# Decoder layer on one core: key norms read from the Gram matrix's diagonal on VectorE, two key products moved inside the first projection, the second state products given a bank of their own

## The chip, the cores and the metric

The kernel runs on one core of a Trainium2 chip. The metric is the device time of one execution in microseconds (us). Five engines work side by side, each through its own list of instructions in order: TensorE (PE in the rows, its weight loads PEld), VectorE (DVE), ScalarE (ACT), GpSimd (POOL), and SyncE (SP), which only issues transfers. They meet through semaphores.

## What is computed

One decoder layer for 4 sequences of 512 tokens with 512 features: a gated delta rule attention with 16 heads, a small cross attention over 64 sets, and a feed-forward part with ternary weights. The change lies in the attention:

```
q = silu(conv(h @ Wq)); k = silu(conv(h @ Wk)); v = silu(conv(h @ Wv))     # DK = 96, DV = 192
q = l2norm(q) * DK ** -0.5;  k = l2norm(k)         # x * rsqrt(sum(x * x) + 1e-6)
beta = 2 * sigmoid(h @ Wb);  g = -exp(A_log) * softplus(h @ Wa + dt_bias)
for every token:
    S = S * exp(g);  delta = (v - k @ S) * beta;  S = S + outer(k, delta);  o = q @ S
o = rmsnorm(o) * norm_weight * silu(h @ Wg);  out = x + o @ Wo
```

The kernel never normalizes the key itself. It divides what is made of the key by sum(k * k) + EPS, so every token needs that sum.

## The kernel before

The attention (`stage_delta_rule`) takes a head's 512 tokens in four chunks of 128, for all four sequences at once. One call of `step(st)` on each engine is one chunk of one head: 64 full steps n, with chunk c = n % 4, written out one after another, with no loop on the chip. A step overlaps the stages of several chunks. It projects and convolves chunk n + 2 (three jobs of 128 features, `projection`, `tap0`, `conv`, `tanh`, `silu`), prepares chunk m = n + 1 ("turn": the key's Gram matrix, the decay differences, the transposes to tokens, the triangular inverse), runs the recurrence on chunk n ("recur"), and projects the output of chunk n - 1.

Each engine's order is written by hand: the calls in TensorE's `step`, and the lists of (condition, function) at the end of ScalarE's and VectorE's `step`. `past` and `hold` are waits on a semaphore for a value.

The places that matter here, in the order of a step:

- `keys(st)`, TensorE. ScalarE's `key_squares` squares the key (96 features x 512 tokens) into the tile `junk`. TensorE multiplies it with a column of ones, four products with one column each (L705), and gets sum(k * k) per token in bank 2. Then four products key by key (L710) fill bank 6 with the Gram matrix of each sequence.
- `exponent_sums(st)`, TensorE (L692): the decay differences into bank 5, which ScalarE's `decay` turns into `E` (L985).
- `keyscale`, VectorE (L1171, L1177, L1183): from the sums in bank 2 it makes `nsse` = -(sum + EPS), its reciprocal, and `Dn` = reciprocal times beta. `masked` (L1259) then makes the lower triangular matrix `LT` = Gram x Dn x E.
- GpSimd: the norm factor of the previous chunk (`ms`, `rn`), then `Gm` for the next decay differences (L592), then `UB` from `Dn` (L599), `Em` (L604), the scaled keys `K2` (L636).
- `y_16` (L737) and `x_16` (L744, L745), TensorE: the first two levels of the inverse. `y_16` waits until the inverse's 16 x 16 blocks have come back through HBM as `X` and `XT` (L550), `x_16` waits for VectorE's `Y16` (L1161). The blocks are inverted on 32 partitions by VectorE's `recursion` late in the step before.
- `add_x(i)`, VectorE (L1309): adds one sequence's projected output to x. The delta products (`V`, `XT`, L800) reuse those banks and wait for it.
- At the end of a step: the state products K2 x Dl (L800), two pairs of sequences, pair 0 into bank 4 and pair 1 into bank 7. Bank 7 still holds the second pair of output gates until VectorE's `gate_pair(1)` (L1238) has read them, so pair 1 waits for that. In chunk 3 there are no state products: the state starts anew with the next head, and VectorE only clears S (L1280). VectorE's order at the end of the step is silu of job 2, `gate_pair(1)`, two `out_pair` (L1247 or L1249), `state` (L1275).

The line numbers are those of the kernel before.

## Time and profile before

| | |
|---|---|
| median of three runs | 2714.29 us (2713.38 to 2724.97) |
| the profiled execution's own time | 2716.69 us |
| its span in the trace | 2714.9 us |
| TensorE busy | 2516.7 us, 93% |
| VectorE busy | 2068.5 us, 76% |
| ScalarE busy | 1362.4 us, 50% |
| GpSimd busy | 900.5 us, 33% |
| attention with all of its stages running (135 to 2150 us): TensorE busy | 1952.2 of 2015.0 us |
| granted TensorE clock there | 0.99 |

The table gives totals. The rows below give places: a row of a timeline is a run of equal instructions with its start in the span and its length, and in square brackets how long its engine stood idle just before it and which instruction ended that. A TensorE row's end is modelled, since matmuls are pipelined, so TensorE's time is best read from the start of one row to the start of the next.

### The profile page before, as it was taken

Reading aid. Unit: us, or ns where it says so; the run is one execution under the profiler, and the core shown is the slowest. Engines: PE = TensorE matmul, PEld = TensorE weight load, DVE = VectorE, ACT = ScalarE, POOL = GpSimd, SP = SyncE. Lnnn points to the kernel's source line nnn. Section 1 sums busy time; section 2 is a strip of 40 time slices with the busy share of each in tenths; the row PEclk is TensorE's granted clock in tenths of the full one; section 3 lists DMA queues with packets and bytes.
Section 4 is the critical chain, followed back from the end, with each engine's and each line's share of the span. In section 5 each row is a group of like instructions: output and inputs, shape, how many; then the busy total and the mean of one; then the engine's idle time right before and its main releaser. Section 6 shows DMA issues by size and latency. Waiting matters only on the chain. (4 is left out here: it accounts for less than half of the span.)

```text
span 2714.9 us, 55951 instructions
## 1 busy us (share of the span) xinstructions
PE 2516.7 (93%) x20408; PEld 1698.7 (63%) x20408; DVE 2068.5 (76%) x5037; ACT 1362.4 (50%) x3171; POOL 900.5 (33%) x1210
## 2 busy tenths in 40 slices
PE   4599999999999999999999999999999999877998
PEld 3367676766666666676666676666666666653443
DVE  6577778887878787878787878788887878456776
ACT  2245455555555555555555555554545444323555
POOL 0223333333333233333333333333333323113544
PEclk8789899999999999999999999999999999687999
DMA  2211111111211111222222222221111010030000
GB/s 86 61 36 47 46 49 47 49 47 49 47 47 45 44 39 38 55 52 56 54 57 55 57 54 57 55 56 34 33 30 31 20 32 18 13 121 1 20 20 24
DMA packets 289341, 120.78 MB, mean 44 GB/s; under 512 B 211462, under 2 KB 267046, under 8 KB 288556
## 3 DMA queue, kind: packets, MB, share of 16 engines
q1 hardware_dynamic: 289068, 117.21, 16.9%
q8 instruction: 163, 2.67, 0.4%
q14 instruction: 110, 0.90, 0.1%
HBM read 85.42 MB, written 31.74 MB: 43 GB/s over the span
## 5 line engine op out<-in xcount | busy, mean ns | idle before, releaser
L1125 DVE SCALAR_TENSOR_TENSOR d_y<-bank,d_cw,d_y 128x508 f32<-128x508 f32 (+2 forms) x576 | 422.6, 734 | 146.3 <-ACT d_y L923 136.5
L622 POOL TENSOR_SCALAR d_ms<-d_sso 128x4 f32<-128x4 f32 x64 | 14.5, 227 | 911.5 <-ACT d_junk L1056 911.5
L642 POOL TENSOR_TENSOR d_sq<-d_tok 128x384 f32<-128x384 f32 x64 | 52.8, 826 | 509.9 <-ACT d_tok L976 509.9
L1041 ACT ACTIVATE d_thg<-bank 128x384 f32<-128x384 f32 x128 | 61.6, 481 | 311.7 <-PE bank L788 311.6
L923 ACT ACTIVATE d_y<-bank,d_cw 128x512 f32<-128x512 f32 x192 | 131.5, 685 | 141.2 <-PE bank L669 140.0
L1309 DVE SCALAR_TENSOR_TENSOR x<-bank,x 128x512 f32<-128x512 f32 x256 | 171.8, 671 | 21.4 <-PE bank L831 21.4
L976 ACT ACTIVATE d_tok<-bank 128x384 f32<-128x384 f32 x256 | 125.5, 490 | 54.0 <-PE bank L684 50.0
L1151 DVE SCALAR_TENSOR_TENSOR d_yv<-d_th,d_y 128x512 f32<-128x512 f32 x128 | 88.9, 694 | 81.0 <-ACT d_th L930 80.4
L930 ACT ACTIVATE d_th<-d_y 128x512 f32<-128x512 f32 x192 | 119.6, 623 | 55.5 <-DVE d_tail L1136 55.4
L636 POOL TENSOR_SCALAR d_K<-d_tok,d_Em 128x96 f32<-128x96 f32 x256 | 144.0, 578 | 0.1
L1133 DVE SCALAR_TENSOR_TENSOR d_y<-d_tail,d_cw,d_y 128x4 f32<-128x4 f32 (+2 forms) x432 | 123.7, 286 | 15.3
L1056 ACT ACTIVATE d_junk<-d_O 128x192 f32<-128x192 f32 x256 | 89.6, 351 | 88.8 <-DVE d_O L1249 66.5
L831 PE MATMUL bank<-d_wo1h,d_onT 128*128 128x512 f16 x384 | 129.5, 392 | 3.5 <-ACT d_onT L1068 3.5
L788 PE MATMUL bank<-d_wgh,hhi 128*128 128x192 f16 x1024 | 127.1, 247 | 0.0
L788 PE MATMUL bank<-d_wgl,hhi 128*128 128x192 f16 x1024 | 126.4, 246 | 0.0
L788 PE MATMUL bank<-d_wgh,hlo 128*128 128x192 f16 x1024 | 126.4, 246 | 0.0
L831 PE MATMUL bank<-d_wo0h,d_onT 128*128 128x512 f16 x384 | 125.7, 382 | 0.0
L614 POOL TENSOR_TENSOR d_V<-d_tok,d_kinv 128x640 f32<-128x640 f32 (+1 forms) x128 | 124.2, 991 | 0.0
L669 PE MATMUL bank<-hhi,d_wa0h 128*128 128x512 f16 x384 | 102.8, 392 | 19.3 <-DVE d_wa0l L1102 16.2
L800 PE MATMUL bank<-d_Dl,d_K 128*96 128x192 f32 x384 | 82.7, 338 | 36.2 <-DVE d_gate L1238 34.4
L1665 POOL TENSOR_TENSOR f_zv<-f_zv,f_zg 128x512 f32<-128x512 f32 x64 | 86.8, 1357 | 86.3 <-DVE f_zv L1831 57.0
L800 PE MATMUL bank<-d_V,d_XT 128*128 128x192 f32 x512 | 108.7, 335 | 6.3 <-DVE x L1309 6.3
(281 smaller groups left out, 7010.1 us busy)
## 6 DMA issues: line engine op xcount, KB each, us to landing
lt_blocks<-d_LT SPq DMA_DIRECT2D x64, 256.0 KB, 2.4
d_fw<-turned_gate_w SPq DMA_DIRECT2D x32, 256.0 KB, 3.2
d_XT<-x_blocks SPq DMA_DIRECT2D x128, 64.0 KB, 2.4
d_X<-x_blocks SPq DMA_DIRECT2D x128, 64.0 KB, 2.5
d_fw<-turned_val_w SPq DMA_DIRECT2D x32, 256.0 KB, 3.2
d_fw<-turned_out_w SPq DMA_DIRECT2D x32, 256.0 KB, 2.9
d_st<-in_L_attn_Wg_dram SPq DMA_DIRECT2D x16, 384.0 KB, 4.7
ternary<-d_ft SPq DMA_DIRECT2D x48, 128.0 KB, 2.1
```

The source lines that it names most:

```text
L614: last = nc.gpsimd.tensor_tensor(V[q][:, :, lo:hi], tok[q][:, :, at:at + hi - lo], over(kinv[:, :], 2, hi - lo), ALU.mult)
L636: nc.gpsimd.tensor_scalar(K2[:, i, :], tok[st.p][:, i, K_AT:K_AT + DK], Em[st.p][:, i, P - 1:P], None, ALU.mult).then_inc(s["K2_ready"], 1)
L669: last = nc.tensor.matmul(acc[:, :], wa[st.wp][w][:, k, t * P:(t + 1) * P], x[:, k, :].rearrange("p (b t) -> p b t", b=B)[:, :, st.cp * P: ...
L788: last = nc.tensor.matmul(bank[(4, 7)[pair]][:, i * DV:(i + 1) * DV], x[:, k, tile * P:(tile + 1) * P], wg[w][:, k, :], start=(e == 0), st ...
L800: last = nc.tensor.matmul(bank[at][0:rows, i * DV:(i + 1) * DV], lhsT(e), rhs(e), start=True, stop=True)
L831: last = nc.tensor.matmul(bank[(4, 7, 6, 5)[i]][:, :], o, w, start=(e == 0), stop=(e == len(terms) - 1))
L923: nc.scalar.activation(y[(st.p + j) % 2][:, :, :].rearrange("p b t -> p (b t)"), bank[(st.p + j) % 2][:, :], ACT.Copy, scale=cw[:, ds(st.k ...
L930: nc.scalar.activation(th[:, :, :], y[(st.p + j) % 2][:, :, :], ACT.Tanh).then_inc(s["tanh_done"], 1)
L976: nc.scalar.activation(tok[st.pm][:, i, :], bank[2][:, 0:QKV], ACT.Copy).then_inc(s["tok_read"], 1)
L1125: nc.vector.scalar_tensor_tensor(out=yy[:, :, tap:], in0=pp[:, :, 0:P - tap], scalar=cw[:, ds(st.kp, 1), t, 3 - tap], in1=yy[:, :, tap:], ...
L1133: nc.vector.scalar_tensor_tensor(out=yy[:, :, 0:back], in0=old[:, :, 3 - back:], scalar=cw[:, ds(st.kp, 1), t, 3 - back], in1=yy[:, :, 0:b ...
L1309: nc.vector.scalar_tensor_tensor(out=xs, in0=bank[(4, 7, 6, 5)[i]][:, :], scalar=1.0 / (SO * SW), in1=xs, op0=ALU.mult, op1=ALU.add).then_ ...
```

## The change

It has three parts. The sums of the squared keys are no longer computed by ScalarE and TensorE: VectorE multiplies the Gram matrix in bank 6 with an identity, into `diag` (the tile `junk` again), and sums each row. The Gram products and the decay differences move up to between the first and second third of the first projection, with VectorE's `keyscale` and `masked` ahead of the convolution, and ScalarE's `decay` ahead of `tap0`. The second pair of state products goes to bank 2, and VectorE's `gate_pair(1)` moves behind `state`. A one-time step for the ternary weights (`magnitudes`) leaves `keyscale` and runs once, later.

```diff
@@ VectorE, keyscale and its place
-                def keyscale(i):
-                    if i == 0:
-                        v.wait_ge(s["key_done"], 2 * m + 1)
-                        nc.vector.tensor_scalar(nsse[:, :], bank[2][:, 3 * P:3 * P + B], EPS, -1.0, ALU.add, ALU.mult).then_inc(s["Dn_ready"], 1)
...
+                def keyscale():
+                    v.wait_ge(s["key_done"], m + 1)
+                    past(v, "ssq_done", B * n)
+                    nc.vector.tensor_tensor(diag, bank[6][:, :].rearrange("p (b t) -> p b t", b=B), over(ident, 1, B), ALU.mult).then_inc(s["Dn_ready"], 1)
+                    v.wait_ge(s["Dn_ready"], 5 * m + 1)
+                    nc.vector.tensor_reduce(nrec[:, :], diag, AXX, ALU.add).then_inc(s["Dn_ready"], 1)
+                    v.wait_ge(s["Dn_ready"], 5 * m + 2)
+                    past(v, "kappa_done", 4 * m - 2)
+                    nc.vector.tensor_scalar(nsse[:, :], nrec[:, :], EPS, -1.0, ALU.add, ALU.mult).then_inc(s["Dn_ready"], 1)
...
-                for go, what in ((P_, lambda: conv(st, 0, 1)), (T_, lambda: keyscale(0)), (T_, lambda: keyscale(1)), (T_, lambda: keyscale(2)),
-                                 (T_, masked), (R_, y16), (P_, lambda: conv(st, 0, 2)), (R_, products), (P_, lambda: conv(st, 0, 3)),
+                for go, what in ((T_, keyscale), (T_, masked), (R_, y16), (P_, lambda: conv(st, 0, 1)), (P_, lambda: conv(st, 0, 2)), (R_, products), (P_, lambda: conv(st, 0, 3)),
...
-                                 (R_, lambda: gate_pair(1)), (R_, lambda: out_pair(0)), (R_, lambda: out_pair(1)), (R_, state)):
+                                 (R_, lambda: out_pair(0)), (R_, lambda: out_pair(1)), (R_, state), (R_, lambda: gate_pair(1))):
@@ TensorE, keys
-                past(pe, "tok_read", B * m)
-                hold(pe, s["ksq_done"], m + 1)
...
-                for i in range(B):
-                    last = nc.tensor.matmul(bank[2][:, 3 * P + i:3 * P + i + 1], ksq[:, i, :], cst[0:DK, C_U + P - 1:C_U + P], start=True, stop=True)
-                last.then_inc(s["key_done"], 1)
+                past(pe, "silu_done", 3 * m + 1)
                 past(pe, "LT_ready", B * m)
                 past(pe, "O_ready", 2 * st.n - 1)
@@ TensorE, queries
                 past(pe, "S_ready", B * n + B)
+                past(pe, "gate_ready", 2 * n)
@@ TensorE, step
-                proj(0)
+                proj(0, 0, 3)
                 if st.turn:
+                    keys(st)
                     exponent_sums(st)
-                    keys(st)
+                proj(0, 1, 3)
+                proj(0, 2, 3)
...
-                if c < CH - 1:
-                    past(pe, "gate_ready", 2 * n + 2)
-                pair_of(st, "su_done", 1, 7, lambda i: K2[:, i, :], lambda i: Dl[:, i, :], rows=DK, product=c < CH - 1)
+                if st.turn:
+                    past(pe, "tok_read", B * n + 2 * B)
+                pair_of(st, "su_done", 1, 2, lambda i: K2[:, i, :], lambda i: Dl[:, i, :], rows=DK, product=c < CH - 1)
@@ ScalarE
-            def key_squares(st):
...
-                nc.scalar.activation(ksq[:, :, :], yv[st.pm][0:DK, 1, :, :], ACT.Square).then_inc(s["ksq_done"], 1)
-                    past(a, "key_done", 2 * n + 3 if st.turn else 2 * n + 1)
+                    past(a, "Dn_ready", 5 * n + 7 if st.turn else 0)
-                for go, what in ((T_, lambda: key_squares(st)), (P_, lambda: tap0(st, 0)), (T_, decay), (True, lambda: heads(0)), (T_, lambda: jobs(0)), (R_, copy_x32), (T_, lambda: tokens(st, 0)),
+                for go, what in ((T_, decay), (P_, lambda: tap0(st, 0)), (True, lambda: heads(0)), (T_, lambda: jobs(0)), (R_, copy_x32), (T_, lambda: tokens(st, 0)),
```

On TensorE, at the border of the second and third full step, the program before has this order. The rows from the state products on (their left operand is `K`, their right one `Dl`, in the rows' names `d_Dl,d_K`) are the end of one step and the start of the next.

```order
L800 MATMUL bank<-d_Dl,d_K 96x192 x4
L669 MATMUL bank<-hhi,d_wa1h 128x512 x4
L669 MATMUL bank<-hhi,d_wa1l 128x512 x4
L669 MATMUL bank<-hlo,d_wa1h 128x512 x4
L692 MATMUL bank<-d_Gm,cst 128x512
L705 MATMUL bank<-cst,d_junk 128x1 x4
L710 MATMUL bank<-d_yv 128x128 x4
L737 MATMUL bank<-d_X,d_LT 64x32 x8
L719 MATMUL bank<-d_qT,d_yv 128x128 x4
```

The changed program has this at the same border.

```order
L798 MATMUL bank<-d_Dl,d_K 96x192 x4
L669 MATMUL bank<-hhi,d_wa1h 128x512 x4
L707 MATMUL bank<-d_yv 128x128 x4
L697 MATMUL bank<-d_Gm,cst 128x512
L669 MATMUL bank<-hhi,d_wa1l 128x512 x4
L669 MATMUL bank<-hlo,d_wa1h 128x512 x4
L735 MATMUL bank<-d_X,d_LT 64x32 x8
L717 MATMUL bank<-d_qT,d_yv 128x128 x4
```

The one-column products are gone, and the Gram products and the decay differences stand two thirds of a projection earlier.

On VectorE, from the last silu of a step (`d_yv<-d_th`) through the first products of the next, the program before has this order.

```order
L1151 SCALAR_TENSOR_TENSOR d_yv<-d_th,d_y 128x512
L1238 SCALAR_TENSOR_TENSOR d_gate<-d_thg,bank 128x384
L1249 TENSOR_TENSOR d_O<-bank,d_Q 128x384 x2
L1275 SCALAR_TENSOR_TENSOR d_S<-d_S,dec,bank 96x192 x4
L1125 SCALAR_TENSOR_TENSOR d_y<-bank,d_cw,d_y 128x4x127
L1171 TENSOR_SCALAR d_nsse<-bank 128x4
L1177 RECIPROCAL d_nrec<-d_nsse 128x4
L1183 TENSOR_TENSOR d_Dn<-d_nrec,sc 128x4
L1259 SCALAR_TENSOR_TENSOR d_LT<-bank,d_Dn,d_E 128x128 x4
L1161 SCALAR_TENSOR_TENSOR d_Y<-bank,cst 128x4x16 x2
L1125 SCALAR_TENSOR_TENSOR d_y<-bank,d_cw,d_y 128x4x126
L1267 TENSOR_TENSOR d_PT<-bank,d_Em 128x512
```

The changed program has this there.

```order
L1144 SCALAR_TENSOR_TENSOR d_yv<-d_th,d_y 128x512
L1245 TENSOR_TENSOR d_O<-bank,d_Q 128x384 x2
L1270 SCALAR_TENSOR_TENSOR d_S<-d_S,dec,bank 96x192 x4
L1234 SCALAR_TENSOR_TENSOR d_gate<-d_thg,bank 128x384
L1163 TENSOR_TENSOR d_junk<-bank,cst 128x512
L1165 TENSOR_REDUCE d_nrec<-d_junk 128x4
L1168 TENSOR_SCALAR d_nsse<-d_nrec 128x4
L1170 RECIPROCAL d_nrec<-d_nsse 128x4
L1172 TENSOR_TENSOR d_Dn<-d_nrec,sc 128x4
L1254 SCALAR_TENSOR_TENSOR d_LT<-bank,d_Dn,d_E 128x128 x4
L1154 SCALAR_TENSOR_TENSOR d_Y<-bank,cst 128x4x16 x2
L1118 SCALAR_TENSOR_TENSOR d_y<-bank,d_cw,d_y 128x4x127
```

The gate stands behind the state update, two instructions are new, and the first tap of the convolution (L1125 before, L1118 now) comes after all of the key's work.

## Rows read from the trace of the kernel before

**Rows 1.** The page: its head, and the engines' busy times.

```profile
span 2714.9 us, 55951 instructions
PE 2516.7 (93%) x20408; PEld 1698.7 (63%) x20408; DVE 2068.5 (76%) x5037; ACT 1362.4 (50%) x3171; POOL 900.5 (33%) x1210
```

**Rows 2.** Timeline of TensorE, end of a chunk 0, start of its chunk 1.

```profile
1291.30 0.89 PE L800 MATMUL bank<-d_Dl,d_K 128*96 128x192 f32 x4 [0.94 <-DVE d_gate L1238]
1292.03 1.03 PE L669 MATMUL bank<-hhi,d_wa0h 128*128 128x512 f16 x4
...
1294.62 1.02 PE L692 MATMUL bank<-d_Gm,cst 128*128 128x512 f32 x2
1295.48 0.95 PE L705 MATMUL bank<-cst,d_junk 96*128 96x1 f32 x8
1296.29 1.14 PE L710 MATMUL bank<-d_yv 96*128 96x128 f32 x8
1297.36 0.66 PE L737 MATMUL bank<-d_X,d_LT 64*64 64x32 f32 x16
...
1299.20 0.31 PE L744 MATMUL bank<-d_Y,d_XT 64*64 64x32 f32 x4
```

**Rows 3.** The page's group of the state products: busy, mean ns | idle before.

```profile
L800 PE MATMUL bank<-d_Dl,d_K 128*96 128x192 f32 x384 | 82.7, 338 | 36.2 <-DVE d_gate L1238 34.4
```

**Rows 4.** Timeline of VectorE over the same border and into chunk 1.

```profile
1291.16 1.02 DVE L1247 COPY d_O<-bank 128x384 f32<-128x384 f32 x2
...
1292.10 1.37 DVE L1275 SCALAR_TENSOR_TENSOR d_S<-d_S,dec,bank 96x192 f32<-96x192 f32 x4
...
1295.60 0.75 DVE L1125 SCALAR_TENSOR_TENSOR d_y<-bank,d_cw,d_y 128x508 f32<-128x508 f32 x1 [2.13 <-ACT d_y L923]
...
1296.88 0.16 DVE L1183 TENSOR_TENSOR d_Dn<-d_nrec,sc 128x4 f32<-128x4 f32 x1
...
1298.68 0.46 DVE L1161 SCALAR_TENSOR_TENSOR d_Y<-bank,cst 128x64 f32<-128x64 f32 x2
...
1299.71 0.68 DVE L1267 TENSOR_TENSOR d_PT<-bank,d_Em 128x512 f32<-128x512 f32 x1
...
1312.35 0.55 DVE L1286 TENSOR_REDUCE d_ss<-d_sq 128x4 f32<-128x384 f32 x1 [0.95 <-POOL d_sq L642]
...
1315.13 0.69 DVE L1151 SCALAR_TENSOR_TENSOR d_qT<-d_th,d_y 128x512 f32<-128x512 f32 x1 [2.04 <-ACT d_th L930]
```

**Rows 5.** Timeline of TensorE in the chunk 0 before it.

```profile
1256.36 1.03 PE L669 MATMUL bank<-hhi,d_wa0h 128*128 128x512 f16 x4
...
1260.88 1.02 PE L705 MATMUL bank<-cst,d_junk 96*128 96x1 f32 x8 [0.78 <-ACT d_junk L954]
...
1284.84 0.89 PE L800 MATMUL bank<-d_V,d_XT 128*128 128x192 f32 x4 [0.42 <-DVE x L1309]
```

**Rows 6.** Timeline of VectorE in that chunk 0.

```profile
1257.37 0.55 DVE L1238 SCALAR_TENSOR_TENSOR d_gate<-d_thg,bank 128x384 f32<-128x384 f32 x1
1257.84 1.02 DVE L1249 TENSOR_TENSOR d_O<-bank,d_Q 128x384 f32<-128x384 f32 x2
...
1262.41 0.32 DVE L1183 TENSOR_TENSOR d_Dn<-d_nrec,sc 128x4 f32<-128x4 f32 x1
1263.12 1.13 DVE L1259 SCALAR_TENSOR_TENSOR d_LT<-bank,d_Dn,d_E 128x128 f32<-128x128 f32 x4 [0.39 <-PE bank L710]
...
1265.19 0.68 DVE L1267 TENSOR_TENSOR d_PT<-bank,d_Em 128x512 f32<-128x512 f32 x1
...
1283.91 0.67 DVE L1309 SCALAR_TENSOR_TENSOR x<-bank,x 128x512 f32<-128x512 f32 x1
```

**Rows 7.** Timeline of GpSimd in that chunk 0.

```profile
1260.08 0.23 POOL L622 TENSOR_SCALAR d_ms<-d_sso 128x4 f32<-128x4 f32 x1 [14.98 <-ACT d_junk L1056]
...
1261.67 1.04 POOL L592 TENSOR_TENSOR d_Gm<-cst,sc 128x512 f32<-128x512 f32 x1
...
1264.30 1.27 POOL L604 TENSOR_TENSOR d_Em<-d_E,d_UB 128x512 f32<-128x512 f32 x1
```

**Rows 8.** SyncE's last load of blocks in chunk 1.

```profile
1292.38 0.62 SPq L550 DMA_DIRECT2D d_X<-x_blocks  x1
```

**Rows 9.** The same in chunk 0.

```profile
1259.00 0.62 SPq L550 DMA_DIRECT2D d_X<-x_blocks  x1
```

**Rows 10.** The page's DMA issues: KB each, median us to landing.

```profile
d_X<-x_blocks SPq DMA_DIRECT2D x128, 64.0 KB, 2.5
```

**Rows 11.** Windows: busy times, PEclk, DMA share, GB/s of two chunk 0 steps.

```profile
275.00:313.50 38.50, 36.36 (x274) 24.74 (x275) 30.05 (x71) 17.40 (x44) 13.52 (x16) 0.82 0.12 31
...
420.00:453.50 33.50, 30.63 (x276) 21.15 (x276) 29.92 (x71) 17.68 (x46) 13.76 (x16) 1.00 0.14 32
```

More of the change, by code:

```diff
@@ L595, in key_decay @@
             def key_decay(m, q):
-                hold(pool, s["Dn_ready"], 3 * m + 3)
+                hold(pool, s["Dn_ready"], 5 * m + 5)
                 past(pool, "Em_ready", m)
@@ L679, in to_tokens @@
                     past(pe, "silu_done", 3 * m + 3)
-                    past(pe, "Dn_ready", 3 * m + 1)
                 past(pe, "tok_read", B * m + i)
+                if i == 0 and st.n == TERN - 1:
+                    past(pe, "fsum_ready", 1)
+                    for e, at in enumerate((C_U, C_GT)):
+                        last = nc.tensor.matmul(bank[2][:, 3 * P + 8:3 * P + 8 + N_W], cst[:, at:at + P], fall[:, :], start=(e == 0), stop=(e == 1))
+                    last.then_inc(s["fgam_done"], 1)
+                    past(pe, "fsum_ready", 2)
                 for t in range(3):
@@ L697, in keys @@
                 m, key = st.n + 1, yv[st.pm][0:DK, 1, :, :]
-                past(pe, "tok_read", B * m)
-                hold(pe, s["ksq_done"], m + 1)
-                if st.n == TERN - 1:
-                    past(pe, "fsum_ready", 1)
-                    for e, at in enumerate((C_U, C_GT)):
-                        nc.tensor.matmul(bank[2][:, 3 * P + 8:3 * P + 8 + N_W], cst[:, at:at + P], fall[:, :], start=(e == 0), stop=(e == 1))
-                for i in range(B):
-                    last = nc.tensor.matmul(bank[2][:, 3 * P + i:3 * P + i + 1], ksq[:, i, :], cst[0:DK, C_U + P - 1:C_U + P], start=True, stop=True)
-                last.then_inc(s["key_done"], 1)
+                past(pe, "silu_done", 3 * m + 1)
                 past(pe, "LT_ready", B * m)
@@ L824, in output @@
                     past(pe, "qs_read", B * n + 2 * i + 2)
-                if i < 2 and st.c == 0:
+                if i < 2 and not st.recur:
                     past(pe, "gate_ready", 2 * n - 1 + i)
@@ L1148, in silu @@
                     past(v, "ks_done", 2 * st.n + 2 if st.recur else 0)
-                    past(v, "ksq_done", st.n + 1)
+                    past(v, "key_done", st.n + 1)
                     dst = yv[st.p][:, t - 1, :, :]
@@ L1185, in square, with magnitudes @@
+                def magnitudes():
+                    v.wait_ge(s["fgam_done"], 1)
+                    nc.vector.tensor_scalar(gam[:, :], bank[2][:, 3 * P + 8:3 * P + 8 + N_W], 1.0 / (FF * D), 1e-5,
+                                            ALU.mult, ALU.max).then_inc(s["fsum_ready"], 1)
+                    v.wait_ge(s["fsum_ready"], 2)
+                    nc.vector.reciprocal(rgam[:, :], gam[:, :]).then_inc(s["gam_ready"], 1)
                 def square(tile, w, row, col):
@@ L1275, in state @@
                             nc.vector.scalar_tensor_tensor(out=S[:, i, :], in0=S[:, i, :], scalar=dec[0:DK, ds(n, 1), i],
-                                                           in1=bank[(4, 7)[i // 2]][0:DK, (i % 2) * DV:(i % 2 + 1) * DV],
+                                                           in1=bank[(4, 2)[i // 2]][0:DK, (i % 2) * DV:(i % 2 + 1) * DV],
                                                            op0=ALU.mult, op1=ALU.add).then_inc(s["S_ready"], 1)
```

32 lines of the change are left out of this document (9 added, 23 removed).

## The prediction, made before the changed kernel was run

> **What bounds the kernel now.** I read the page first. TensorE is busy for 93% of the span and VectorE for 76% [rows 1], and in the attention TensorE's rows follow each other almost without a gap. So I look for two things: TensorE work that goes away, and the few places where TensorE stands idle. Then I ask of the others only whether they are still in time when TensorE comes earlier.
>
> The timeline of TensorE at the start of a chunk 1 shows both. The second pair of state products begins after 0.94 us idle, which VectorE's gate ended. From the one-column products (1295.48) to the Gram products (1296.29) 0.81 us pass, and to the next row, 1297.36, 1.07 us more [rows 2]. The page's group of the state products adds the idle up: 36.2 us over the run, 34.4 of it ended by the gate [rows 3]. It occurs in chunks 0, 1 and 2.
>
> VectorE in the same stretch has room: 2.13 us idle before its first tap, and again 0.95 and 2.04 us before it takes up the second silu [rows 4]. In chunk 0 it is otherwise. There the delta products of TensorE stand idle for 0.42 us until VectorE's `add_x` [rows 5]. VectorE has little room, since it also makes two low halves of weights in that chunk. So TensorE paces chunks 1 to 3, and VectorE the middle of chunk 0.
>
> **The change part by part.** *The one-column products.* They go, in 63 full steps that prepare a next chunk: 63 x 0.81 = 51.0 us.
>
> *The second state pair.* It no longer waits for the gate. Its new wait, for the tokens that were read from bank 2, was met long before. That frees 36.2 us, if nothing else is late next.
>
> *What VectorE must now do, in chunk 1.* The two outputs start where the gate stood, 0.46 us earlier, at 1290.7. By the row starts the state follows 0.94 us later, at 1291.6, and ends 1.37 us after that, at 1293.0. The gate (0.55, as in [rows 6]) ends at 1293.5. Only then comes the new work, which the trace doesn't show. The nearest row to the product with the identity is `PT`, a product of one bank with one tile over 512 columns: 0.68 us. The nearest to the sum is the reduce over 384 columns: 0.55 us, by columns 0.73 for 512 [rows 4]. Low end for the two together: 1.2, if both hide part of their start behind each other. High end: 3.5, if each stands behind one GpSimd instruction of 1.04 [rows 7]. I take 1.4, the rows' own times, since `PT` ran in 0.68 beside GpSimd's `Em` [rows 6, 7]. That is 1294.9. The small ones take some 0.2 us each, so `Dn` is there at 1295.5, `LT` 1.1 later [rows 6], `Y16` 0.46 after that: 1297.1.
>
> *What TensorE asks of it.* The projection starts at 1292.03 - 0.94 = 1291.1. One third of 2.59 is 0.86, then the Gram products 1.07, the decay differences 0.86 (1294.62 to 1295.48), and the other two thirds 1.73: `y_16` begins at 1295.6 instead of 1297.36. `x_16`, which needs `Y16`, comes 1.84 later, at 1297.4 [rows 2]. VectorE is in time by 0.3 us. So its 1.4 us are hidden, in idle time that was 2.13 us; without that cover they cost 1.4 us a step, 88 us in all. Behind `Y16` stand all three taps, but the 0.95 and 2.04 us of idle further on take them up [rows 4].
>
> *A collision.* In chunk 0, `Dn` took 0.32 us and ended at 1262.73, just as GpSimd's `Gm` did (1261.67 + 1.04 = 1262.71); in chunk 1, beside no such row, it took 0.16 [rows 4, 6, 7]. It has two inputs in SBUF. Now `Dn` comes earlier and so meets `Gm` in each chunk: some 0.25 us of the 0.3 in chunk 1. By the Trainium skill, page "SBUF — State Buffer", section "Who interferes with whom", a VectorE instruction with two SBUF inputs is blocked by a GpSimd instruction that reads SBUF, one with at most one such input outside the two-port modes is not. The trace agrees in `Dn` and `PT`; by that rule the identity product and the sum, each with one SBUF input, would not be held.
>
> *The blocks' return.* The last load in chunk 1 is issued at 1292.38 and lands 2.5 later, at 1294.9, before `y_16` at 1295.6 [rows 8, 10]. In chunk 0 it is 1259.00 + 2.5 = 1261.5 [rows 9, 10], against a `y_16` at 1261.6 (below). That is near, but not late.
>
> *Chunk 0.* TensorE is through the first third at 1256.36 + 0.86 = 1257.2 [rows 5]. The Gram products now need bank 6, which the first output frees at 1257.37 + 0.55 = 1257.9 [rows 6]: 0.7 us of new wait, where before 0.78 us went by before the one-column products [rows 5]. These two cancel. With 1.07 + 0.86 + 1.73 `y_16` stands at 1261.6. VectorE's `Dn` lies behind `Gm`, which itself starts some 0.4 earlier (the squares of the output on ScalarE follow the output): 1262.3 against 1262.73. But the first tap, which stood ahead of it, now stands behind, with 0.7. So `PT` begins as before, within 0.2 us, and so do the second half's instructions, `add_x` among them. TensorE, some 0.8 us early, waits for it at the delta products and gives back 0.6 us: 15 x 0.6 = -9 us. After that wait its next gain, the second state pair, counts fully.
>
> *Once.* The ternary scales move behind VectorE's `w_pair`, and TensorE's first transposes of that step wait for them: -1.6 us. ScalarE loses `key_squares` and gains nothing. It is not on the path outside chunk 0.
>
> *The sum.* 51.0 + 36.2 - 9 - 1.6 = 76.6 us. From the profiled execution's 2716.7 us (span 2714.9) that gives 2640.1. The median stands 2.4 us below the profiled execution, so I predict 2638 us.
>
> **The rivals.** *The removed products were nearly free* (0.10). They had one column each, and their 0.81 us could be time in which the array only waits for weights that another group would then wait for. For it speaks that eight passes of one column can hardly fill 0.81 us. Against it: the Gram group behind has its own weights, and the same spacing of about 0.1 to 0.13 us a pass [rows 2]. A quarter left, 63 x 0.2 = 13 us, gives 2676. The Trainium skill, page "TensorE: Matmul & The Clock Gate", section "Wait — 56ns, not 53.3ns?", puts the smallest spacing of matmuls at about 25 ns, so eight would cost 0.2 us and 63 steps 12.6 us; the row says 0.81, and I go by the row.
>
> *VectorE's new pair lands behind GpSimd* (0.14). `rn` and `Gm` run just then. One such row, 1.04 us [rows 7], less what is in hand, makes `x_16` wait about 0.8 in chunks 1 and 2 and 0.5 in chunk 3, whose border gains less, and delays VectorE by 0.8 in chunk 0: 2.9 us a head, 46 us, 2684. `PT` beside `Em` speaks against it.
>
> *More* (0.12). If VectorE's idles in chunk 0 (0.39 before `LT` [rows 6]) absorb more than I think, the 9 us stay. And the state pair's idle is counted from a modelled end: the pair's row is 0.89 long, yet the next begins 0.73 after it [rows 2], so each of 48 waits may have been 0.16 longer, 7.7 us in all. Both together: 2621.
>
> *Slower: the clock falls* (0.05). Two chunk 0 steps of the same kind took 38.50 and 33.50 us, at a mean granted clock of 0.82 and 1.00: in the first TensorE spent part of the stretch at 1.2 GHz instead of 2.4 [rows 11]. A fall costs 5.0 us. What set it off I can't read from the rows. The changed chunk 0 bunches its waits: 0.7 before the Gram products, more than 1 before the delta products. If that brings a fall in each of 15 chunks 0, the 75 us are gone (2713); from the 16th on it is slower, and with every second chunk 1 as well (23 falls) it would be 2753. Against it: TensorE's waits elsewhere shrink.
>
> *No change* (0.03): the state pair's wait comes back in full at `y_16`, for blocks that land later, and the rest in chunk 0.
>
> **How the numbers follow.** The forecast, 2624 to 2650, has 0.56. Its own spread is that of either half of the case of more, and of a wait of 0.2 us at `x_16` in 60 steps. Below it lies that case in full with 0.12, above it the two partial gains with 0.24. From 2618 to 2684 I leave out the clock, the no-change case and the tails, less than 2 in 10. 0.5% is 13.6 us, about what a measurement of this kernel tells from no change, so faster means below 2700.7: 0.93. The clock case divides, and gives slower 0.04, same 0.03.
>
> **What would show it.** In the changed trace: no idle before the second state pair; 0.86 us from the first projection row to the Gram products in chunks 1 to 3; the identity product at 0.68 and the sum near 0.7; `Dn` ending where `Gm` ends; `x_16` without more than 0.2 us of wait; and in chunk 0 a wait of a good 1 us before the delta products, where it was 0.42. A head (four steps) should take 4.9 us less. I am wrong if `x_16` waits for `Y16` by half a microsecond or more, if `y_16` waits for the blocks, or if the granted clock leaves 1.00 in the middle of the attention.

## The result, and the profile after

The changed kernel takes 2633.36 us (median of 4 runs, 2629.04 to 2639.26), the kernel before in the same comparison 2713.93 us (2713.38 to 2724.97). The ratio is 0.9695, with an interval of 0.9663 to 0.9727. The forecast was 2638 us in a range of 2618 to 2684. The profiled execution took 2630.96 us.

The head of the page, beside [rows 1]:

```profile
span 2629.2 us, 54834 instructions
PE 2435.9 (93%) x19896; PEld 1631.3 (62%) x19896; DVE 2179.0 (83%) x5165; ACT 1325.9 (50%) x3107; POOL 903.6 (34%) x1210
```

The span is 85.7 us shorter. TensorE's busy time is down by 80.8 us at the same share, and VectorE's is up by 110.5: it now makes the key's sums that ScalarE and TensorE made.

The timeline of TensorE at the border into a chunk 1 answers to [rows 2]:

```profile
1241.70 1.46 PE L798 MATMUL bank<-d_Dl,d_K 128*96 128x192 f32 x8
1243.00 1.03 PE L669 MATMUL bank<-hhi,d_wa0h 128*128 128x512 f16 x4
1243.87 1.06 PE L707 MATMUL bank<-d_yv 96*128 96x128 f32 x8
1244.76 1.02 PE L697 MATMUL bank<-d_Gm,cst 128*128 128x512 f32 x2
...
1247.44 0.65 PE L735 MATMUL bank<-d_X,d_LT 64*64 64x32 f32 x16
1248.03 1.16 PE L717 MATMUL bank<-d_qT,d_yv 96*128 96x128 f32 x8
1249.77 0.31 PE L742 MATMUL bank<-d_Y,d_XT 64*64 64x32 f32 x4 [0.58 <-DVE d_Y L1154]
```

Both state pairs are now one row of eight, with no idle inside. The projection starts 1.30 us after the first of them. The Gram products follow 0.87 us later. But the last line has a bracket that [rows 2] did not have: `x_16` stands idle for `Y16`.

VectorE in the same stretch, beside [rows 4]:

```profile
1243.79 1.38 DVE L1270 SCALAR_TENSOR_TENSOR d_S<-d_S,dec,bank 96x192 f32<-96x192 f32 x4
1245.08 0.54 DVE L1234 SCALAR_TENSOR_TENSOR d_gate<-d_thg,bank 128x384 f32<-128x384 f32 x1
1245.55 0.68 DVE L1163 TENSOR_TENSOR d_junk<-bank,cst 128x512 f32<-128x512 f32 x1
1246.26 0.69 DVE L1165 TENSOR_REDUCE d_nrec<-d_junk 128x4 f32<-128x512 f32 x1
1246.98 0.78 DVE L1168 TENSOR_SCALAR d_nsse<-d_nrec 128x4 f32<-128x4 f32 x1
1247.79 0.18 DVE L1170 RECIPROCAL d_nrec<-d_nsse 128x4 f32<-128x4 f32 x1
1248.01 0.16 DVE L1172 TENSOR_TENSOR d_Dn<-d_nrec,sc 128x4 f32<-128x4 f32 x1
1248.20 1.13 DVE L1254 SCALAR_TENSOR_TENSOR d_LT<-bank,d_Dn,d_E 128x128 f32<-128x128 f32 x4
1249.24 0.47 DVE L1154 SCALAR_TENSOR_TENSOR d_Y<-bank,cst 128x64 f32<-128x64 f32 x2
```

and GpSimd, beside [rows 7]:

```profile
1245.68 1.04 POOL L627 TENSOR_TENSOR d_rn<-d_ms,d_mhalf 128x4 f32<-128x4 f32 x1
1246.69 1.04 POOL L592 TENSOR_TENSOR d_Gm<-cst,sc 128x512 f32<-128x512 f32 x1
```

Read the two together. `nsse` has four columns and takes 0.78 us; it ends at 1247.76, and `Gm` ends at 1247.73. In chunk 0 it is `Dn` (1214.39, 0.76 us, to 1215.15) that ends with `Gm` (1215.14). The product with the identity (0.68) and the sum (0.69), which lie beside `rn` and `Gm` as well, are not held.

TensorE's waits over the attention (135 to 2250 us; total us, times, longest):

```profile
PE bank L742 <- DVE d_Y L1154: 20.5, 42, 0.9
PE bank L707 <- DVE d_O L1245: 10.6, 16, 0.7
PE bank L751 <- ACT d_XT L989: 6.6, 14, 0.6
PE bank L798 <- DVE x L1304: 6.3, 15, 0.4
PE bank L735 <- DMA d_X<-x_blocks: 5.2, 12, 1.2
```

The gate's wait of [rows 3] is off the list but for one of 2.7 us at the start. `x_16` (L742) waits in its place, for 20.5 us. The last line is new as well: `y_16` now waits at times for the blocks to come back, where the kernel before had no such wait.

GpSimd's L622 runs once a step and serves as a clock for all that follows: I take the distance from one to the next as the length of a step, and the median of each of the four kinds over the middle of the attention. The same head, before and after:

```profile
1293.41 0.23 POOL L622 TENSOR_SCALAR d_ms<-d_sso 128x4 f32<-128x4 f32 x1 [12.93 <-ACT d_junk L1056]
...
1433.35 0.23 POOL L622 TENSOR_SCALAR d_ms<-d_sso 128x4 f32<-128x4 f32 x1 [12.93 <-ACT d_junk L1056]
```

```profile
1245.10 0.23 POOL L622 TENSOR_SCALAR d_ms<-d_sso 128x4 f32<-128x4 f32 x1 [12.46 <-ACT d_junk L1049]
...
1379.70 0.23 POOL L622 TENSOR_SCALAR d_ms<-d_sso 128x4 f32<-128x4 f32 x1 [12.46 <-ACT d_junk L1049]
```

That is 139.94 and 134.60 us; with the medians 139.93 and 134.60, 5.33 a head, 85.3 us in 16 heads, which is the whole difference of the spans.

**Where it came from.** From row starts of TensorE, the median of each of the three borders inside a head, before and after in microseconds:

| stretch of a border | chunk 0 to 1 | 1 to 2 | 2 to 3 |
|---|---|---|---|
| first state pair to projection | 2.48, 1.30 | 2.35, 1.30 | 1.69, 1.30 |
| projection to `y_16` | 5.33, 4.44 | 5.33, 4.44 | 5.33, 4.44 |
| `y_16` to `x_16` | 1.84, 2.33 | 1.84, 2.20 | 1.84, 1.67 |
| `x_16` to the products with the state | 1.07, 1.07 | 1.07, 1.07 | 1.07, 1.07 |

The borders differ, so each is counted by itself. They gain 1.58, 1.56 and 1.45 us: in a head 2.62 from the state pair and 2.67 from the stretch to `y_16`, less 0.68 at `x_16`, together 4.6. Some 0.7 are left for chunk 0, whose step takes 32.60 instead of 33.34 us.

### The profile page after: what moved, and what is told of

It is laid out like the page before. It is cut to its first block and busy times, and to the rows that moved or that the text cites. A ratio compares the mean times of both kernels' runs of the same rounds, so it can differ in the third digit from the quotient of the medians.

```text
span 2629.2 us, 54834 instructions
## 1 busy us (share of the span) xinstructions
PE 2435.9 (93%) x19896; PEld 1631.3 (62%) x19896; DVE 2179.0 (83%) x5165; ACT 1325.9 (50%) x3107; POOL 903.6 (34%) x1210
## 5 line engine op out<-in xcount | busy, mean ns | idle before, releaser
L1118 DVE SCALAR_TENSOR_TENSOR d_y<-bank,d_cw,d_y 128x508 f32<-128x508 f32 (+2 forms) x576 | 422.6, 734 | 20.8 <-ACT d_y L923 9.2
L622 POOL TENSOR_SCALAR d_ms<-d_sso 128x4 f32<-128x4 f32 x64 | 14.5, 227 | 879.9 <-ACT d_junk L1049 879.9
L1039 ACT ACTIVATE d_Dl<-bank 128x384 f32<-128x384 f32 x128 | 62.9, 492 | 97.0 <-PE bank L798 97.0
```

The costliest lines, as they stand in the source:

```text
L1118: nc.vector.scalar_tensor_tensor(out=yy[:, :, tap:], in0=pp[:, :, 0:P - tap], scalar=cw[:, ds(st.kp, 1), t, 3 - tap], in1=yy[:, :, tap:], ...
```

## The experiments

All times are medians of a comparison with runs of the kernel before on the same chip, and a ratio stands only where there were several runs. The kernel before stood at 2725.88 us in the comparison of the first four experiments, at 2714.04 in that of the next four and at 2716.88 in that of the last three, so ratios, and not times, are to be compared between these groups. Since single executions differ by some tens of microseconds where TensorE's granted clock falls in some steps, the length of a head (four step medians, as above) is the sharper measure, and I give both.

**The state pair alone** (`bank2_only`). The kernel before, with the second pair in bank 2 and the gate behind the state (VectorE's read of the bank and three of TensorE's waits follow and are left out here):

```diff
-                if c < CH - 1:
-                    past(pe, "gate_ready", 2 * n + 2)
-                pair_of(st, "su_done", 1, 7, lambda i: K2[:, i, :], lambda i: Dl[:, i, :], rows=DK, product=c < CH - 1)
+                if st.turn:
+                    past(pe, "tok_read", B * n + 2 * B)
+                pair_of(st, "su_done", 1, 2, lambda i: K2[:, i, :], lambda i: Dl[:, i, :], rows=DK, product=c < CH - 1)
...
-                                 (R_, lambda: gate_pair(1)), (R_, lambda: out_pair(0)), (R_, lambda: out_pair(1)), (R_, state)):
+                                 (R_, lambda: out_pair(0)), (R_, lambda: out_pair(1)), (R_, state), (R_, lambda: gate_pair(1))):
```

> The kernel before with one part of the change: the second state pair goes to bank 2 and VectorE's gate_pair(1) stands behind state; keys, products and projection stay as they were. My theory: the wait of 0.94 us (chunk 0 to 1), 0.81 (1 to 2) and a little (2 to 3) goes, 36 us over the run, perhaps 44 if the modelled ends hide 0.16 of each; nothing takes its place, since VectorE had 2.13 us idle behind state. Time 2714 - 36 to 44 = 2670 to 2678. Rival: the wait only moves (to the delta products of chunk 0, to the blocks' return or to Y16), and less than 15 us is gained: above 2699.

Measured: 2694.49 us (5 runs), ratio 0.9899 (0.9859 to 0.9939), span 2690.1, 24.8 less than before. The head is 136.87 us, 3.06 less, which makes 49 us in 16 heads. The two numbers differ by falls of the clock. The windows of a chunk 0 step with one and of one without (width; busy us of each engine; granted clock; DMA share, GB/s):

```profile
547.00:585.00 38.00, 37.17 (x276) 24.32 (x275) 29.59 (x69) 17.57 (x44) 13.52 (x16) 0.82 0.13 31
...
685.00:718.00 33.00, 31.40 (x278) 21.00 (x277) 29.57 (x70) 17.95 (x45) 13.76 (x16) 1.00 0.14 36
```

Six steps of this execution are 5.2 to 5.7 us longer than their kind, 32.5 us in all; in the kernel before it was two, 8.4 us. 24.8 + 32.5 - 8.4 = 48.9. So the part is worth 49 us, and this execution gave half of it back to the clock. Of the 49, 42 lie at the borders (1.18, 1.05 and 0.39 a head, as in the table) and 7 in chunk 0, whose step gains 0.46: with the gate moved, VectorE's outputs, ScalarE's squares behind them and the one-column products that wait for those come earlier.

**The keys and the order alone** (`keys_only`). The changed kernel, with the second pair in bank 7 behind the gate again, the edit above in reverse.

> The changed kernel with the state pair's part undone: pair 1 in bank 7 again, gate_pair(1) ahead of the outputs, and pair 1 waits for it. My theory: the two parts add up, so this stands 36 to 44 us above the changed kernel's 2633, at 2669 to 2677. Rival: they overlap. The outputs on VectorE start later here, and so the squares on ScalarE and GpSimd's Gm, while the Gram products come when they come; if the key's chain then meets less of GpSimd, x_16 waits less than 0.4 us a step and this comes out at 2660 or below.

Measured: 2670.05 us (4 runs), ratio 0.9793 (0.9746 to 0.984); head 136.54, 3.39 less, 54 us in 16 heads. The wait for the gate is back (window 135 to 2300 us), and both rows belong to one view:

```profile
PE bank L798 <- DVE d_gate L1234: 32.5, 40, 2.6
...
PE bank L742 <- DVE d_Y L1154: 5.5, 13, 0.6
```

Together the two parts alone save 6.45 us a head, the full change 5.33. The second row says where the other 1.1 went: with TensorE held at the gate, `Y16` is in time (5.5 us in 13 waits, and 1.67 us from `y_16` to `x_16` at each border), although `nsse` is held there too (0.64 us); with both parts in, the first two borders take 2.33 and 2.20, and that is 1.2 us.

**The one-column products back, in the changed kernel** (`onecol_back`), into bank 6, where the Gram products write over them:

```diff
                 for i in range(B):
+                    nc.tensor.matmul(bank[6][:, i:i + 1], key[:, i, :], cst[0:DK, C_U + P - 1:C_U + P], start=True, stop=True)
+                for i in range(B):
                     last = nc.tensor.matmul(bank[6][:, i * P:(i + 1) * P], ...)
```

> The changed kernel with four one-column products per step put back on TensorE, ahead of the Gram products, into bank 6, where the Gram products then overwrite them: the output stays the same, only their time on TensorE is back. By the row of before they cost 0.81 us a step, 51 us over 63 steps. But in the changed kernel TensorE waits 0.4 to 0.6 us for Y16 at x_16 in chunks 1 to 3, because a small VectorE instruction ends with GpSimd's Gm, not because of the Gram products. If that is right, this wait absorbs most of it: only 0.2 to 0.4 us a step in chunks 1 to 3 are lost and the wait at x_16 nearly goes, 15 to 25 us in all, 2648 to 2658. Rival A: the Gram products' time sets Y16: full 0.81 a step, 2684, with the wait at x_16 as it was. Rival B: such products cost about 0.2 us a step whatever follows: 13 us, with x_16's wait shorter by the same 0.2 alone.

Measured: 2658.45 us (4 runs), ratio 0.9752 (0.9712 to 0.9792); head 136.52, 1.92 more than the changed kernel, 30.7 us in 16. The timeline of TensorE at its border shows why it isn't 0.81 a step:

```profile
1263.64 0.95 PE L707 MATMUL bank<-cst,d_yv 96*128 96x1 f32 x8
1264.45 1.14 PE L709 MATMUL bank<-d_yv 96*128 96x128 f32 x8
...
1268.69 1.16 PE L719 MATMUL bank<-d_qT,d_yv 96*128 96x128 f32 x8
1269.78 0.31 PE L744 MATMUL bank<-d_Y,d_XT 64*64 64x32 f32 x4
```

The products occupy 0.81 us again, and the wait at `x_16` is gone. They fill time in which TensorE would have stood idle. By steps they cost 0.23 us at the first border, 0.37 at the second, 0.89 at the third, where there was no wait, and 0.43 in chunk 0.

**`Gm` behind `Em` on GpSimd** (`gm_late`), so that nothing of GpSimd lies beside the small instructions:

```diff
-                if st.project:
-                    exponents(n + 2)
                 if st.turn:
                     key_decay(m, st.pm)
+                if st.project:
+                    exponents(n + 2)
```

> The changed kernel with GpSimd's Gm (for the next step's decay differences) moved behind Em: nothing else moves. My theory: the 0.78 us that the scale instruction nsse takes in chunk 1 (and Dn's 0.76 in chunk 0) are a wait for Gm, which ends at the same moment. Without it nsse takes some 0.2 us, Y16 comes 0.5 us earlier, and the waits of TensorE at x_16 (21 us over the run) fall below 5 us: 2613 to 2620. Rival A: the key's chain on VectorE is long by itself, Y16 stays late, and this is within 5 us of the changed kernel. Rival B: with x_16 early TensorE waits for the blocks at y_16 in the next steps instead, and half of the gain is lost: 2624.

Measured: 2619.12 us (4 runs), ratio 0.9595 (0.955 to 0.9641); head 133.35, 1.25 less than the changed kernel. VectorE and TensorE at the border:

```profile
1240.70 0.17 DVE L1168 TENSOR_SCALAR d_nsse<-d_nrec 128x4 f32<-128x4 f32 x1
...
1241.12 0.16 DVE L1172 TENSOR_TENSOR d_Dn<-d_nrec,sc 128x4 f32<-128x4 f32 x1
...
1242.36 0.47 DVE L1154 SCALAR_TENSOR_TENSOR d_Y<-bank,cst 128x64 f32<-128x64 f32 x2
```

```profile
1243.24 0.31 PE L742 MATMUL bank<-d_Y,d_XT 64*64 64x32 f32 x4
```

`nsse` takes 0.17 us and not 0.78, and `x_16` has no wait. From `y_16` to `x_16` it is 1.72, 1.67 and 1.67 us at the three borders, where the changed kernel has 2.33, 2.20 and 1.67 and the kernel before 1.84. That settles the cause of the 20.5 us. The first two borders get 1.14 of the 1.25 us, chunk 0 only 0.12. And what is left is no reserve: `Y16` ends 6.11 us after the projection's first row (1236.72 to 1242.83), and `x_16` is free to start 4.44 + 1.67 = 6.11 after it.

**The same, with the one-column products** (`gm_late_onecol`): the last two edits together, to price the products where nothing absorbs them.

> The kernel with Gm moved behind Em, and the four one-column products per step put back into bank 6 ahead of the Gram products, where these overwrite them. There TensorE no longer waits at x_16, so nothing can absorb them. Theory: each step gets 0.81 us longer, a head of four steps goes from 133.35 to 136.6 us, and the x_16 wait stays at nothing. Rival B (such products cost 0.2 us a step): 134.2. Rival C (Gm is not what delays the key's chain): the chain slips with the Gram products and waits at x_16 appear again.

Measured: 2654.13 us (one run; before 2714.04). The head is 136.45 against 133.35: 3.10 us. Chunk 0 pays 0.48 of it (32.48 to 32.96) and each border inside the head 0.89: from projection to `y_16` it is 5.33 us again, against 4.44. The row of before said 0.81; the Gram products behind take 0.98 to the next row (1264.45 to 1265.43 in `onecol_back`) instead of 0.89, and that makes the rest. In `onecol_back` the head is the same within 0.1 us, and `y_16` to `x_16` is 1.67 in both: with the products in, it makes no difference whether `Gm` collides. No run has the Gram products and the decay differences in their old place without the one-column products, so what the earlier place is worth in the changed kernel is not shown. With the one-column products in, the new order (`onecol_back`, 136.52) is 0.35 us a head shorter than the old one (`bank2_only`, 136.87).

**One small instruction less** (`one_small_less`). `Gm` stays where the change has it, but the epsilon goes into the identity product and the sign into `Dn`, so that `nsse` as a `tensor_scalar` is gone (GpSimd's `sse`, made from it, changes its sign too):

```diff
-                    nc.vector.tensor_tensor(diag, bank[6]..., over(ident, 1, B), ALU.mult)
+                    nc.vector.scalar_tensor_tensor(out=diag, in0=bank[6]..., scalar=EPS, in1=over(ident, 1, B), op0=ALU.add, op1=ALU.mult)
-                    nc.vector.tensor_reduce(nrec[:, :], diag, AXX, ALU.add)
...
-                    nc.vector.tensor_scalar(nsse[:, :], nrec[:, :], EPS, -1.0, ALU.add, ALU.mult)
+                    nc.vector.tensor_reduce(nsse[:, :], diag, AXX, ALU.add)
...
-                    nc.vector.tensor_tensor(Dn[:, :], nrec[:, :], sc[:, BETA, ds(m, 1), :].squeeze(1), ALU.mult)
+                    nc.vector.scalar_tensor_tensor(out=Dn[:, :], in0=nrec[:, :], scalar=-1.0, in1=sc[:, BETA, ds(m, 1), :].squeeze(1), op0=ALU.mult, op1=ALU.mult)
```

> The changed kernel, Gm where it was, with EPS added in the identity product (from PSUM, scalar_tensor_tensor) and the sign in Dn: the instruction nsse (one input in SBUF, tensor_scalar) is gone, and VectorE makes four instead of five for the key's scale. It tells what Gm holds up. If it holds up whatever small instruction comes then, the reciprocal now takes its 0.78 us in chunk 1 and the x_16 wait falls only by some 0.2 of 0.53 us. If it holds up instructions with two SBUF inputs and this form of tensor_scalar, but not a reciprocal or a reduce, then the reciprocal takes 0.18, Dn (two inputs) ends with Gm, and the x_16 wait falls by 0.4 in chunk 1, to some 0.1 us; a head goes from 134.6 to about 133.6.

Measured: 2620.12 us (one run); head 133.78, 0.82 less than the changed kernel, so it mends two thirds of what `gm_late` does. VectorE, and GpSimd's `Gm`:

```profile
1241.39 0.69 DVE L1167 TENSOR_REDUCE d_nsse<-d_junk 128x4 f32<-128x512 f32 x1
1242.11 0.18 DVE L1169 RECIPROCAL d_nrec<-d_nsse 128x4 f32<-128x4 f32 x1
1242.32 0.50 DVE L1171 SCALAR_TENSOR_TENSOR d_Dn<-d_nrec,sc 128x4 f32<-128x4 f32 x1
```

```profile
1241.77 1.04 POOL L592 TENSOR_TENSOR d_Gm<-cst,sc 128x512 f32<-128x512 f32 x1
```

The reduce and the reciprocal run in the middle of `Gm` at their usual length. `Dn`, with two inputs in SBUF, is held to its end (1242.82, `Gm` 1242.81).

**`Gm` last of all on GpSimd** (`gm_last`): `exponents(n + 2)` moves behind `epsq`, GpSimd's last instruction of a step.

> The changed kernel with Gm as GpSimd's last instruction of a step, behind epsq. In the kernel with Gm behind Em, chunk 0 gained only 0.1 us, and there the three tail instructions of VectorE (two inputs in SBUF) took 1.22 instead of 0.75 us while Gm ran. Theory: with Gm out of that place too the tails take 0.75, VectorE's chunk 0 is 0.5 us earlier, and the head is 0.3 to 0.5 us shorter than 133.35. Rival: chunk 0 is set elsewhere (the wait for the output's bank, the copies before y_32), and the head stays at 133.3.

Measured: 2605.87 us (one run); head 133.11, 0.24 less than `gm_late`, all of it in chunk 0 (32.21 against 32.48). The median hides that these steps are no longer alike: seven of fifteen take 32.03 to 32.05 us, seven 32.1 to 32.9, and n = 24 takes 37.2. Why, no run shows.

**Spare products in the waits of a chunk 0, on `bank2_only`** (`bank2_filled`). TensorE multiplies two 512-column groups into a bank that is written over, once ahead of the one-column products and once ahead of the delta products, in each chunk 0. The question was whether TensorE's idle there sets off the falls.

```diff
+                if st.recur and st.c == 0:
+                    past(pe, "LT_ready", B * m)
+                    for _ in range(2):
+                        nc.tensor.matmul(bank[6][:, :], wa[0][0][:, 0, 0:P], hhi[:, 0, 0:512], start=True, stop=True)
...
+                if c == 0:
+                    for _ in range(2):
+                        nc.tensor.matmul(bank[3][:, :], wa[0][0][:, 0, 0:P], hhi[:, 0, 0:512], start=True, stop=True)
```

> The kernel before with the second state pair in bank 2 alone, and in every chunk 0 two spare products of 512 columns ahead of the one-column products and two ahead of the delta products, in the places where TensorE waited 0.42 and 0.37 us; they write banks that are overwritten and change no output. In the run without them the granted clock fell to 1.2 GHz in four chunks 0 for 13.7 us each, at 5.2 us a fall, and the median was 2694 where the heads alone give 2667. Theory: these waits bring the falls on; filled, there are none in the middle of the attention and the ratio to before is 0.982 or below instead of 0.990. Rival: the falls come regardless, some four of them stay in the profile, and the ratio stays near 0.990.

Measured: 2664.02 us (4 runs, 2649.54 to 2671.98), ratio 0.9798 (0.9742 to 0.9853), against 0.9899 for `bank2_only`. The head is nearly the same (136.63 and 136.87). In the profiled execution one step's clock falls (n = 40, 38.4 us), where it was six. The two come from different chips, so this is an indication and no more.

**The changed kernel once more** (`changed_again`), in one comparison with the next two.

> The changed kernel itself, unedited, so that the two versions after it can be compared with it in the same rounds. Ratio to before 0.970 as at first; its spread (2629 to 2639 us) comes from clock falls, 3 to 6 us each, that come in some chunks 0 and not in others.

Measured: 2642.3 us (6 runs, 2631.62 to 2648.06), ratio 0.9708 (0.9666 to 0.9749); head 134.62. The granted clock left 1.00 in six steps of the middle here, for 3.4 to 10.2 us each, and in two in the first profile. With the longer steps out, the head is the same as in the first profile (134.60), so the two executions differ by the clock and not by their work.

**All three repairs** (`all_three`): `gm_last`, `one_small_less`, and the ternary scales (`magnitudes`) back behind `y16`, early enough for TensorE's transposes. The two products of TensorE that they need move up as well, behind the decay differences; of this edit only VectorE's part is shown.

```diff
-                                 (R_, lambda: w_pair(1)), (n == TERN - 1, magnitudes),
+                                 (R_, lambda: w_pair(1)),
...
-                for go, what in ((T_, keyscale), (T_, masked), (R_, y16),
+                for go, what in ((T_, keyscale), (T_, masked), (R_, y16), (n == TERN - 1, magnitudes),
```

> The changed kernel with Gm as GpSimd's last instruction of a step, EPS added in the identity product (one small VectorE instruction less), and the ternary scales' two products back beside the decay differences, with VectorE's part behind Y16. Gm last alone gave a head of 133.1 us against 134.6 and a span of 2604. Theory: in chunks 1 to 3 TensorE waits nowhere at x_16, so one instruction less brings nothing there and up to 0.2 us in chunk 0; the step with the ternary scales (n = 24) takes 33 instead of 37 to 39 us, and the clock fall beside it goes: 2597 to 2603, ratio to before 0.957 to 0.960. Rival: the fall at n = 24 is not caused by the 2 us wait and stays, 2604.

Measured: 2606.89 us (6 runs, 2600.14 to 2611.33), ratio 0.9577 (0.9537 to 0.9616); head 133.15. Beside 2642.3 on the same chip it beats the changed kernel by 35 us, and their intervals do not meet. The head is that of `gm_last`: with `Gm` out of the way, one small instruction less brings nothing. The step with the ternary scales (n = 24), in the changed kernel, with an ordinary chunk 0 step beside it:

```profile
943.00:975.90 32.90, 30.31 (x211) 19.95 (x212) 26.25 (x62) 13.54 (x36) 8.47 (x10) 0.84 0.05 8
...
1077.90:1110.50 32.60, 31.07 (x275) 21.00 (x273) 30.97 (x73) 18.63 (x43) 13.96 (x17) 1.00 0.18 45
```

and in `all_three`:

```profile
930.00:963.00 33.00, 31.96 (x280) 21.56 (x279) 31.18 (x76) 16.29 (x41) 13.18 (x17) 1.00 0.14 30
```

The wait and the fall are both gone.

**The same with spare products** (`all_three_filled`), three 512-column groups ahead of the Gram products and two ahead of the delta products.

> The same kernel with spare products of 512 columns in chunk 0, three in the wait before the Gram products and two in the wait before the delta products, into bank 3, which is overwritten later; the output stays the same. Theory: the waits of TensorE in chunk 0 bring the clock falls on; with 1.1 us of them filled the falls in the middle of the attention go, the heads keep their length within 0.2 us, the runs lie within 5 us of each other and the median is at or below that of the kernel without them. Rival A: the spare products push work behind them and cost 0.2 us or more a head, 3 us and up. Rival B: falls come regardless, with the same spread.

Measured: 2607.9 us (6 runs, 2597.84 to 2619.44), ratio 0.9582 (0.954 to 0.9625); head 133.08; one fall, at n = 22. No gain.

## Why the prediction was right, and where it was not

The total is right to 4.6 us, and part of that is luck. The working's sum of 76.6 us starts from a profiled execution and gave 2640.1 us for the next one; it took 2630.96, and terms that were too low by 18 us stand there against one that was too high by 11. Of the prediction's own three signs of being wrong all three came: `x_16` waits for `Y16` by 0.58 us in chunk 1, `y_16` waits for the blocks (12 times, 5.2 us), and the granted clock left 1.00 in the middle of the attention. By its steps:

*The one-column products, 51.0 us.* Right: 3.10 us a head when they are put back where nothing waits, 49.6 us in 16 heads. The rival that they were nearly free fell: eight one-column passes take 0.81 us from start to start, 0.10 each. The Trainium skill, page "TensorE: Matmul & The Clock Gate", section "Wait — 56ns, not 53.3ns?", gives about 25 ns as the spacing below which matmuls never come. The trace does not contradict that floor, but these passes stand four times as far apart, so 0.2 us for eight was no estimate of their cost. What sets the 0.10 no run shows; each pass has 128 columns of weights of its own. By borders the cost is distributed otherwise than I had it: 0.89 in each of three, and 0.48 in chunk 0, where TensorE waits for VectorE's output ahead of the Gram products anyway.

*The second state pair, 36.2 us.* The mechanism is right, the term too small: 16 x 2.62 = 42 us at the borders, and 7 more in chunk 0 by `bank2_only`. I read the idle in brackets, and it is counted from modelled ends. At the border of [rows 2] the first pair, whose row is

```profile
1289.55 0.81 PE L800 MATMUL bank<-d_Dl,d_K 128*96 128x192 f32 x4
```

to the projection at 1292.03 took 2.48 us, now 1.30: 1.18 gained, with 0.94 in the bracket. At the second border it is 1.05 with 0.81, at the third (1361.19 to 1362.88 before) 0.39 with 0.15: each bracket is 0.24 short. The prediction had this as a part of its case of more, at 0.16 a wait. The 36.2 also held 5.2 us of the first step, 2.7 of which are still there.

*VectorE's new pair, 1.4 us.* Right: 0.68 and 0.69, and neither held by GpSimd. The rival that it lands behind GpSimd fell for the pair and came true for `nsse` and `Dn`, which stand behind it.

*`x_16` with 0.3 us in hand, no more than 0.2 of wait.* This is the step that failed most. `x_16` waits 0.58 us in chunk 1, 0.45 in chunk 2, 0.41 in chunk 0 (medians) and hardly in chunk 3, 20.5 us in all; `y_16` to `x_16` grew from 1.84 to 2.33 and 2.20 at the first two borders. I charged the collision with `Gm` only to `Dn`, because only `Dn` was known to have two inputs in SBUF, at 0.25 us. In chunks 1 and 2 the instruction that met `Gm` was `nsse`, held from 0.17 to 0.78 us; in chunk 3 it was held too (0.56), without a wait of TensorE. And the 0.3 us in hand were the difference of two estimates of 1297: `gm_late` shows that there was nothing in hand. `gm_late` shows the cause: with `Gm` away, the wait goes. `bank2_only` and `keys_only` show that it took back 1.1 us a head of what the parts save apart. A little of it was an error in my favour: without any wait the stretch is 1.67 us, so the 1.84 of before held 0.17 of waiting that I took for work.

*Chunk 0 gives back 9 us.* Wrong: I had left 15 x 0.81 - 9 = 3 us to it, and it gains 15 x 0.74 = 11. Of the 0.74 `bank2_only` alone gains 0.46, which I had at nothing. I expected the wait before the delta products to grow past 1 us. It is 0.41 [rows 5]:

```profile
1209.23 1.03 PE L669 MATMUL bank<-hhi,d_wa0h 128*128 128x512 f16 x4
...
1210.95 1.13 PE L707 MATMUL bank<-d_yv 96*128 96x128 f32 x8 [0.69 <-DVE d_O L1245]
...
1236.99 0.89 PE L798 MATMUL bank<-d_V,d_XT 128*128 128x192 f32 x4 [0.41 <-DVE x L1304]
```

From the projection to the delta products it was 28.48 us before (1256.36 to 1284.84), now 27.76. TensorE gained 0.72 on this way, and the wait at its end did not grow. The wait of 0.7 before the Gram products came as foretold (10.6 us in 16). What I missed, as far as the rows show it, is that VectorE in chunk 0 does not run on a time of its own. Further on its tail instructions stand behind a GpSimd product that itself follows TensorE's transposes:

```profile
1227.29 1.92 DVE L1126 SCALAR_TENSOR_TENSOR d_y<-d_tail,d_cw,d_y 128x4 f32<-128x4 f32 x3
```

```profile
1226.79 0.83 POOL L642 TENSOR_TENSOR d_sq<-d_tok 128x384 f32<-128x384 f32 x1 [4.69 <-ACT d_tok L969]
1227.58 1.61 POOL L614 TENSOR_TENSOR d_V<-d_tok,d_kinv 128x640 f32<-128x640 f32 x2
```

They end together, 1229.21 and 1229.19. In the kernel before the same pair ended at 1277.05 and 1277.03:

```profile
1274.88 2.17 DVE L1133 SCALAR_TENSOR_TENSOR d_y<-d_tail,d_cw,d_y 128x4 f32<-128x4 f32 x3
```

```profile
1275.42 1.61 POOL L614 TENSOR_TENSOR d_V<-d_tok,d_kinv 128x640 f32<-128x640 f32 x2
```

The tail instructions have two inputs in SBUF; three of them took 0.76 us where no such product lay beside them (1252.42, in chunk 1). From the projection's start `V` stands 19.06 us away before and 18.35 after, 0.71 less, which is TensorE's 0.72. So when TensorE comes earlier, the tokens, `V` and with them VectorE come earlier too. No experiment moved `V`, so this is argued and not shown; the ends that meet in both kernels and the two distances are the evidence.

*Once, 1.6 us.* The wait is there, at 2.0. The ternary scales' step is 38.61 us against 32.60 of its kind. Of these 6.0 us 2.0 are the wait:

```profile
945.23 0.48 PE L689 MATMUL bank<-cst,d_qT 128*128 128x128 f32 x1 [2.01 <-DVE gam L1176]
```

The rest is a fall of the granted clock of 10.2 us that begins within it (943.7), and the granted clock over the window is 0.84. In all eight profiled executions with the scales late the clock left 1.00 in this step, in four of the five with them early (the kernel before, `bank2_filled`, `all_three`, `all_three_filled`) it did not; in `bank2_only`, the fifth, it did, as in four other chunks 0.

*The clock.* The slower rival's trigger was wrong: the changed chunk 0 has the 0.7 us before the Gram products, yet the clock falls in two of the middle steps, n = 24 and n = 52, as in the kernel before in two (n = 1 and 4). A fall costs 3 to 6 us, about the 5.0 of the forecast. But `bank2_only` shows that the rival was not far off: there it falls in five of 15 chunks 0, for 5 us and more each. With spare products it fell in one, on another chip, and in `all_three_filled` they did nothing. All five runs of `bank2_only` have a lower mean granted clock (0.951 to 0.956) than the eight of the kernel before beside them (0.957 to 0.968), so its falls are not the chance of one execution. What sets these falls off is open.

The sum then reads, in microseconds: state pair 16 x 2.62 = 42, projection to `y_16` 16 x 2.67 = 43, `y_16` to `x_16` 16 x -0.68 = -11, chunk 0 15 x 0.74 = 11, and the longer steps 8.4 before against 9.1 after, -1. That makes 84 of the 85.7. In the same order the prediction had 36, 48 x 0.81 = 39, 0, 12 - 9 = 3 and -1.6. Too low were the state pair (by 6), the stretch to `y_16` (by 4) and chunk 0 (by 8), too high the freedom at `x_16` (by 11).

## What to carry to other kernels

When TensorE comes earlier, take what it then waits for by name, and give each small instruction of that chain the length of the longest GpSimd instruction that can lie beside it: here an instruction of 0.17 us cost 0.78, and moving one GpSimd product, with no work changed, was worth 1.25 us a head, 20 us in all. Measure a stall from start to start against an unstalled group of the same shape; at the border shown the bracket said 0.94 of 1.18 us. Where places of one kind differ, count each kind by itself: 48 times the middle of the three borders would have made 50 us of the state pair's 42. And before charging an engine with falling behind, check whether its own waits follow the engine that comes earlier.
